# One graph layer on one core: a prelude with statistics of two rows at once, other chunks and other GpSimd shares, and an opening that runs two blocks ahead of the second unit's gather, with 22 units in place of 21

## What is computed

```python
# x (12500, 128) f32; src, dst (200000,) int32, sorted by dst
h   = relu(layernorm(x))                       # eps 1e-5
agg = segment_sum(h[src], dst, 12500) / max(deg, 1)[:, None]
h1  = relu(agg @ Wg + h @ Ws + bg)             # 128 -> 128
h2  = tanh(h1 @ W1 + b1)                       # 128 -> 512
h3  = tanh(h2 @ W2 + b2)                       # 512 -> 512
out = x + h3 @ W3 + b3                         # 512 -> 128
```

## Time and profile before

| what | value |
|---|---|
| median of 3 runs | 1659.8 us (1656.84 to 1665.99) |
| the profiled execution's own time | 1658.69 us |
| its span | 1656.8 us |
| TensorE busy | 1257.9 us, 76% of the span |
| VectorE, GpSimd, ScalarE busy | 956.5, 897.7, 552.8 us |
| mean granted TensorE clock | 0.904 of full speed |

### The profile page before, as it was taken

The page is one execution under the profiler, slowest core; times in us unless marked ns, Lnnn a source line. Parts: engine busy times, 40 slices in busy tenths (PEclk is TensorE's granted clock), DMA queues, the critical chain, the costliest instruction groups (busy, mean ns, idle before and its releaser), DMA issues.

```text
span 1656.8 us, 26502 instructions
## 1 busy us (share of the span) xinstructions
PE 1257.9 (76%) x9082; PEld 924.4 (56%) x9082; DVE 956.5 (58%) x1850; ACT 552.8 (33%) x1159; POOL 897.7 (54%) x953
## 2 busy tenths in 40 slices
PE   0204988778887888877888788888887888887888
PEld 0202656556665656565655555666555656565667
DVE  8806985546555575646556574547555665546441
ACT  6303441414142341414142341424142432324152
POOL 4473165656555655656566554656555554565530
PEclk9557999999989999888999999999988889899999
DMA  9611224142413314141414313141313313141410
GB/s 244 190 51 62 79 62 100 49 99 64 87 42 100 94 44 99 45 99 41 104 49 100 92 46 93 47 102 44 103 45 101 91 45 94 47 102 43 101 41 10
DMA packets 92829, 130.44 MB, mean 79 GB/s; under 512 B 47451, under 2 KB 73393, under 8 KB 88993
## 3 DMA queue, kind: packets, MB, share of 16 engines
q1 hardware_dynamic: 63773, 69.42, 16.3%
q0 software_dynamic: 28928, 59.30, 14.4%
HBM read 109.14 MB, written 13.09 MB: 74 GB/s over the span
## 4 chain that ended last, share of the span: by engine, by line
PE 54%; another core or an unknown queue 18%; issue 12%; ACT 8%; DVE 6%; DMA 1%; DVEq 0%; SPq 0%; ACTq 0%
PE banks L870 16%; PE banks L816 14%; PE banks L741 7%; PE banks L832 5%; PE banks L853 4%; PE banks L887 4%; DVE arena L1584 3%; ACT arena L1204 2%; ACT dense L1187 2%; ACT arena L1125 1%; PE banks L844 1%; PE banks L847 1%; ACT dense L1194 1%; PE banks L789 1%
## 5 line engine op out<-in xcount | busy, mean ns | idle before, releaser
L669 POOL DMA_INDIRECT ring<-h_table,idx_all x904 | 875.6, 969 | 670.3 <-issue 235.7
L870 PE MATMUL banks<-dense,w 128*128 128x256 f32 (+1 forms) x1568 | 430.5, 392 | 30.1 <-ACT dense L1194 16.8
L816 PE MATMUL banks<-xin,arena 128*128 128x256 f16 x2058 | 313.5, 287 | 103.9 <-issue 61.3
L1204 ACT CAST arena<-banks 128x512 f16<-128x512 f32 (+1 forms) x525 | 291.7, 579 | 206.2 <-PE banks L816 129.8
L870 PEld LDWEIGHTS banks<-dense,w 128*128 128x128 f32 x1568 | 272.2, 197 | 76.7 <-ACT dense L1194 20.8
L816 PEld LDWEIGHTS banks<-xin,arena 128*128 128x128 f16 x2058 | 190.3, 102 | 217.8 <-issue 117.4
L741 PE MATMUL banks<-ring,onehot 128*128 (+1 forms) x1008 | 194.6, 290 | 23.9 <-issue 18.1
L1574 DVE TENSOR_SCALAR arena<-arena,code_ptr 128x768 f16<-128x768 f16 (+1 forms) x336 | 133.6, 456 | 119.0 <-PE banks L816 89.6
L1584 DVE TENSOR_TENSOR arena<-node,banks 128x768 f16<-128x768 f16 (+1 forms) x168 | 152.5, 965 | 45.9 <-remote 24.7
L1194 ACT ACTIVATE dense<-banks,b2c 128x256 f32<-128x256 f32 (+1 forms) x196 | 92.0, 475 | 243.5 <-PE banks L870 125.7
L832 PE MATMUL banks<-arena 64*128 64x257 f16 x2058 | 146.5, 288 | 27.1 <-issue 21.5
(11 more groups left out here) (121 smaller groups left out, 871.2 us busy)
## 6 DMA issues: line engine op xcount, KB each, us to landing
arena<-unit_codes SPq DMA_DIRECT2D x21, 1568.0 KB
ring<-h_table,idx_all POOLq DMA_INDIRECT x904
xblk<-in_x_dram SPq DMA_DIRECT2D x48, 128.0 KB
out_dram<-dense SPq DMA_DIRECT2D x48, 128.0 KB
xin<-in_x_dram SPq DMA_DIRECT2D x4, 1232.0 KB, 17.0
h_table<-xin SPq DMA_DIRECT2D x4, 1232.0 KB
own_pair<-h_table SPq DMA_TRANSPOSE x98
w<-in_L_gnn_W_dram SPq DMA_DIRECT2D x1, 1024.0 KB
```

The source lines that it names most:

```text
L669: nc.gpsimd.indirect_dma_start(out=ring_tiles[:, t % RING, 0:2 * D], out_offset=None, in_=table, in_offset=bass.IndirectOffsetOnAxis(ap=id ...
L816: mm = nc.tensor.matmul(to, wide_l[:, piece % WSLOTS, k, j, :], tab[:, row_of(g, j), :], start=(j == 0), stop=(j == 1))
L870: mm = nc.tensor.matmul(l3_ps[c][:, 0:w], w2[:, q, c * P:(c + 1) * P], h2T[:, q, 0:w], start=(q == 0), stop=(q == HC - 1))
L1204: nc.scalar.copy(unit_msgs[:, 2 * pr:2 * pr + wide_of, 0:2 * D], unit_ps[pr % 2][:, 0:wide_of * 2 * D].rearrange("p (g d) -> p g d", d=2 * ...
```

## The change

It does the following.
- **Prelude.** Six chunks of 10, 22, 22, 18, 16 and 10 rows. `bn_stats` reads two rows at once, element by element in turn, so that its even and odd statistics are those of the two rows; the four joining instructions go. GpSimd scales 6, 12, 12, 10, 9 and 5 rows (54 of 98, before 36). GpSimd's memset of the part of x that has no rows goes, and SyncE's wait for it; other rows of x are loaded there. All of `take_idx` now follows the last chunk.
- **Opening.** Once unit 0 is gathered it is summed at once. Then its block goes through the dense layers with the steps 0 and 1 (`first_block`), and unit 1 is placed behind them. Then GpSimd's block 0 goes through the layers beside the gather of unit 1 (`first_gather`), and then unit 1's block alone beside the gather of unit 2 (`period_alone`). The second part of `split_sources`, before placed in the wait for unit 0's codes, now follows unit 0's `residual`.
- **Division.** `PB` = 27: 27 GpSimd blocks (before 28) and 22 units (before 21). `EXTRA_BEHIND` has six entries (before eight). The number of full periods (a GpSimd block and a unit's block) stays 18, from n = 3 to 20, before from n = 2 to 19; the last period is as before.

```diff
@@ -32,7 +32,10 @@
 ROWS = 22
 ROWS_OF = 98
 LAST_OF = 54
-POOL_ROWS = 8
+CHUNKS = ((0, 10), (10, 32), (32, 54), (54, 72), (72, 88), (88, 98))
+POOL_ROWS = (6, 12, 12, 10, 9, 5)
+EDGES_BEHIND = 3
+CAST_BEHIND = 3
 GT = 8
 RG = 8
 RING = RG * GT
@@ -44,8 +47,8 @@
 SUB = 128
 W = 18
 REACH = 22
-PB = 28
-EXTRA_BEHIND = (2, 4, 7, 9, 12, 14, 17, 19)
+PB = 27
+EXTRA_BEHIND = (4, 8, 12, 15, 18, 20)
 TH = 18
 UT = 2 * TH
 UCH = 2
@@ -59,10 +62,12 @@
 FIRST_UC = 100
 PAIRS_BETWEEN = (1, 1, 2, 1, 2, 2, 1, 2, 1, 1, 2, 1, 2, 1, 1, 2)
 PAIRS_ALONE = (2, 2, 2, 2, 2, 2, 2, 2, 2, 2, 2, 1, 0, 0, 0, 0)
+PAIRS_FIRST = (0, 0, 0, 0, 0, 0, 1, 1, 2, 2, 2, 2, 2, 2, 2, 2)
 AHEAD = 18
 CARRY_SLOT = 6
 TURN_SLOT = 13
 CARRY_ALONE = 3
+CARRY_FIRST = 10
 ARENA = 29320
 SCALE = 1024.0
 FAR = 32.0
@@ -128,10 +134,13 @@
 
         return m >= PB
 
-    PERIODS, EXTRA, ORDER, pool = [((), [])], {}, [], 0
+    PERIODS, EXTRA, ORDER, pool = [((0, 1), [PB])], {}, [PB], 0
     for n in range(1, UNITS):
         if n == 1:
-            PERIODS.append(((0, 1), [PB]))
+            PERIODS.append(((2,), [0]))
+            pool = 1
+        elif n == 2:
+            PERIODS.append(((3,), [PB + 1]))
         else:
             PERIODS.append(((2 * pool + 2, 2 * pool + 3), [pool, PB + n - 1]))
             pool += 1
@@ -644,17 +653,15 @@
                            allow_small_or_imprecise_dtypes=True).then_inc(iota_ready, 1)
             pool.wait_ge(iota_ready, 5)
             pool.wait_ge(ident_ready, 2)
-            nc.gpsimd.memset(xin[P - 32:P, LAST_OF:ROWS_OF], 0.0).then_inc(tail_zero, 1)
-            pool.wait_ge(tail_zero, 1)
 
             for c in range(TC):
                 s = c % 2
-                p, rows, held = chunk_rows(c)
+                _first, _rows, held = chunk_rows(c)
                 at(pool, pair_ready, c - 1)
                 pool.wait_ge(shift_ready, c + 1)
-                for r in range(min(POOL_ROWS, rows // 2 - 1)):
-                    ins = nc.gpsimd.tensor_scalar(hval[0:p, s, r, 0:D], held[0:p, r], scale[0:p, s, r:r + 1],
-                                                  shift[0:p, s, r:r + 1], ALU.mult, ALU.add)
+                for r in range(POOL_ROWS[c]):
+                    ins = nc.gpsimd.tensor_scalar(hval[:, s, r, 0:D], held[:, r], scale[:, s, r:r + 1],
+                                                  shift[:, s, r:r + 1], ALU.mult, ALU.add)
                 ins.then_inc(pool_scaled, 1)
 
             table_whole(pool)
@@ -922,14 +929,37 @@
             def end_period(n):
 
                 following = behind(n)
-                if is_unit(following):
-                    sum_unit(n, range(NP))
-                else:
-                    before_turn = WSLOTS if n == 1 else 0
-                    sum_unit(n, range(before_turn))
-                    turn(PLACE[following])
-                    sum_unit(n, range(before_turn, NP))
-                    layer1(following, PLACE[following])
+                turn(PLACE[following])
+                sum_unit(n, range(NP))
+                layer1(following, PLACE[following])
+
+            def first_block():
+
+                steps, (block,) = PERIODS[0]
+                following = PERIODS[1][1][0]
+                leads = {}
+
+                def beside_layer3(slot):
+                    if slot == 7:
+                        leads[1] = begin_sums(steps[1])
+                    if slot >= 7:
+                        sum_tiles(steps[1], leads[1], range(min(2 * (slot - 7), W), min(2 * (slot - 6), W)))
+
+                def beside_out(slot):
+                    if slot == NT * HC - 1:
+                        for c in range(UCH):
+                            place_chunk(1, c)
+
+                turn(0)
+                layer1(block, 0)
+                leads[0] = begin_sums(steps[0])
+                sum_tiles(steps[0], leads[0], range(W))
+                layer2(block, 0)
+                layer3(block, 0, beside_layer3)
+                layer4(0, 2, beside_out)
+                turn(PLACE[following])
+                turn_codes(1)
+                layer1(following, PLACE[following])
 
             def extra_block(n):
 
@@ -954,12 +984,33 @@
                 layer4(k, n + 2)
                 layer1(following, PLACE[following])
 
+            def first_gather(n):
+
+                (step,), (block,) = PERIODS[n]
+                k = PLACE[block]
+                behind_layers = sum(PAIRS_FIRST)
+
+                def beside_layer3(slot):
+                    if slot == CARRY_FIRST:
+                        carry_groups(n + 1)
+                    pr = sum(PAIRS_FIRST[:slot])
+                    gather_pairs(n, range(pr, pr + PAIRS_FIRST[slot]))
+
+                layer2(block, k)
+                layer3(block, k, beside_layer3)
+                layer4(k, n + 2)
+                gather_pairs(n, range(behind_layers, PAIRS))
+                for c in range(UCH):
+                    place_chunk(n + 1, c)
+                segment(step)
+                turn_codes(n + 1)
+                sum_unit(n, range(NP))
+
             def period_alone(n):
 
-                steps, (unit,) = PERIODS[n]
+                (step,), (unit,) = PERIODS[n]
                 k = PLACE[unit]
-                if steps:
-                    segment(steps[0])
+                segment(step)
                 turn(k)
                 layer1(unit, k)
                 layer2(unit, k)
@@ -1084,12 +1133,12 @@
             gather_pairs(0, range(PAIRS // 2 + 1))
             carry_groups(1)
             gather_pairs(0, range(PAIRS // 2 + 1, PAIRS))
-            for c in range(UCH):
-                place_chunk(1, c)
-            turn_codes(1)
-            end_period(0)
+            sum_unit(0, range(NP))
+            first_block()
             for n in range(1, UNITS):
                 if n == 1:
+                    first_gather(n)
+                elif n == 2:
                     period_alone(n)
                 elif n < UNITS - 1:
                     period(n)
@@ -1315,40 +1394,31 @@
 
             def norm_stats(c):
                 s = c % 2
-                p, rows, held = chunk_rows(c)
-                dve.wait_ge(x_in[c], 16 * len(chunk_parts(c)))
-                for r in range(rows):
-                    ins = nc.vector.bn_stats(stats[0:p, s, r], held[0:p, r])
-                ins.then_inc(stats_done, 1)
-                dve.wait_ge(stats_done, c + 1)
-                halves = [stats[0:p, s, 0:rows, k:k + 2] for k in (1, 4)]
-                nc.vector.tensor_tensor(pair_sums[0:p, s, 0:rows], halves[0], halves[1], ALU.add)
-                nc.vector.tensor_tensor(apart[0:p, s, 0:rows], halves[0][:, :, 0], halves[1][:, :, 0], ALU.subtract
-                                        ).then_inc(spread_done, 1)
-                dve.wait_ge(spread_done, 2 * c + 1)
-                nc.vector.scalar_tensor_tensor(out=variance[0:p, s, 0:rows], in0=apart[0:p, s, 0:rows], scalar=D / 4.0,
-                                               in1=apart[0:p, s, 0:rows], op0=ALU.mult, op1=ALU.mult).then_inc(spread_done, 1)
-                dve.wait_ge(spread_done, 2 * c + 2)
-                nc.vector.tensor_tensor(variance[0:p, s, 0:rows], variance[0:p, s, 0:rows], pair_sums[0:p, s, 0:rows, 1], ALU.add
-                                        ).then_inc(moments_done, 1)
+                _first, rows, held = chunk_rows(c)
+                dve.wait_ge(x_in[c], 16 * len(x_parts(c)))
+                for r in range(0, rows, 2):
+                    ins = nc.vector.bn_stats(stats[:, s, r:r + 2].rearrange("p r k -> p (r k)"),
+                                             held[:, r:r + 2].rearrange("p r d -> p d r"))
+                ins.then_inc(moments_done, 1)
 
             def norm_shift(c):
                 s = c % 2
-                p, rows, held = chunk_rows(c)
+                _first, rows, _held = chunk_rows(c)
...
@@ -1652,25 +1722,46 @@
                 if s + 2 < STEPS:
                     make_onehot(s + 2)
 
-            def period_alone(n):
-
-                steps, (unit,) = PERIODS[n]
+            def first_gather(n):
+
+                (step,), (block,) = PERIODS[n]
+                k = PLACE[block]
                 match_codes(n, [4])
                 count_earlier(n + 1)
                 match_codes(n, [5])
                 load_edges(n + 1)
                 match_codes(n, [6, 7])
-                finish(steps[0])
                 rank_edges(n + 1)
                 spread_ranks(n + 1, range(UCH))
-                make_onehot(steps[1])
                 match_nodes(n, range(WSLOTS))
-                residual(PLACE[unit])
-                add_own(PLACE[unit] + 1)
-                finish(steps[1])
+                add_own(k + 1)
+                residual(k)
+                finish(step)
                 match_nodes(n, range(WSLOTS, NP))
-                make_onehot(steps[0] + 2)
-                make_onehot(steps[1] + 2)
+                take_nodes(n + 1)
+                finish_unit(n)
```

(71 more changed lines are left out.)

180 lines of the change are left out of this document (103 added, 77 removed).

## The result

The changed kernel takes 1673.4 us (median of 5 runs, 1671.0 to 1681.8) against 1659.8 (5 runs, 1656.3 to 1666.0): ratio 1.0117, 95% interval 1.0074 to 1.016, so 12 to 27 us slower. Forecast: 1675. The profiled execution is the slowest of the five (1681.8; span 1680.0 against 1656.8), so what follows adds up to +23.2 us, not to the medians' +13.6.

The account below looks back on a forecast made before the run. No engine is full; TensorE and its hand-overs bound the middle. Prelude 0, opening +62.2 and extras -43.6 give +18.6, or +15.8 with gathers priced apart; +16.3 taken on 1658.7 gives 1675 us, range 1652 to 1692.

Parts of the forecast that it names:

- the simple way: Whole kernel: prelude 0, opening +62.2, two extra blocks fewer at 21.8 us each -43.6; sum +18.6 us.
- the second way: Whole kernel: gathers priced apart at 0.4 to 0.5 us, an extra block without its surplus gathers at 16.8; sum +15.8 us.
- The middle: Full periods: 18 stay as they are, two extra blocks go; -43.6 us, or -33.6 - 25 with gathers priced apart.
- The opening: From unit 0's gather to the first full period's layer 2: 73.1 to 135.3 us, +62.2, for two more blocks.
- The prelude: Statistics and norms before the gathers: last `norm_low` moves by -2.2 to +3.0 us; 0 taken.
- the walk through the six chunks: Prelude: chunks followed through VectorE, ScalarE and DMA; last `norm_low`, before at 59.0, ends at 56.8 or 62.0 us.
- the cheap price: Prelude: each of 49 two-row statistics takes 0.33 us, 16.3 us in all, 3.1 less than before.
- the dear end: Prelude: statistics at 0.59 us each, the interleaved read paying for line changes; +3.0 us, given one chance in two.
- The gap: Between unit 0's `place_chunk` matmuls and ScalarE's `take_q`: 53.5 us without progress of layers or units, length kept.
- the rival that it might shrink: Gap ahead of `take_q`: shrinks with the shifted start, deciding from 25 us; whole, 1622 us; nearly all of faster's 0.13.
- the opening pays for itself: Opening: overlaps like a full period and costs 50 to 53 us, total 1663 to 1666; no change, chance 0.20.
- the opening is worse: Opening: gathers and idle slow TensorE to clock 0.92, 82% busy; 135 us become 152, total 1692; chance 0.10.

Follow-up runs that it names:

- div22: The kernel before with the new division alone (27 GpSimd blocks, 22 units, six extras), old prelude and opening: 1665.5 us, ratio 1.0036.
- after_split: The changed kernel with the second `split_sources` moved back into VectorE's long wait for unit 0's codes, ahead of `take_nodes(0)`: 1672.0 us, ratio 1.0072 to the kernel before.
- after_hold13_o24: The changed kernel with GpSimd stopped behind 13 gathers until unit 0's codes, and OPEN_LOTS 24 (later gathers each await TensorE's leave): 1643.9 us, 0.9917 of the kernel before.
- hold13_24: The kernel before with GpSimd's gathers stopped behind 13 until unit 0's codes and behind 24 until unit 1's: 1652.8 us, ratio 0.9979.
- before_late: The kernel before with GpSimd issuing no gather until unit 0's codes are there: 1661.9 us, ratio 1.0036.
- after_rows: The changed kernel with fewer prelude rows for GpSimd, POOL_ROWS (3, 8, 8, 6, 5, 3): run once for its trace, 1681.1 us.

## Why the prediction was right, step by step

**The sign and the size** came from one comparison that held: two extra blocks leave the middle cheaply, and two blocks in the opening are dear. Forecast +16.3; measured +13.6 by the medians, 12 to 27 by the ratio. But both big terms of the simple way were too small, the opening by 17.9 us and the middle by 17.1. That these errors cancelled was luck in that way; the second way had both larger, for one reason, the gathers.

**The middle** was -43.6 by the simple way and -58.6 with gathers priced by themselves; it came to -60.7. The price of an extra (88 us a window) held; the windows without one fell from 66.3 to 64.7 us, with 36.6 gathers in place of 40. That is 0.5 us a gather, the price of the second way, and div22 shows that it comes with the division. The first way, which I listed first, sized it wrong: an extra's surplus gathers were paid by its neighbours, one of the signs of being wrong that the prediction names. Its 55 to 57 gathers a window with an extra don't fit all seven: counted by their starts they are 50 to 56, with a mean of 52.7, and 36 to 43 in the ten without, with a mean of 40.

**The opening** was +62.2, or +74 by the second way, and came to +80.1. Unit 0's layer 2 came 33.5 us behind the gather's start (forecast 31.6). `place_chunk(1)` took 4.4 us in place of 1.0, single matmuls 0.7 us apart beside gathers; block 0's layer 2 ran at half clock, 3.78 us; the idle ahead of unit 1's first pair was 4.5 us (forecast 7, and after_split shows its named cause right). Unit 1's layer 2 came at +105.4 (forecast 97.6). The largest miss is the period behind it: 47.8 us where I took 37.7, because I carried over unit 0's period as it was. That had 9 gathers beside it, this one has 24; 15 more at the second way's 0.4 to 0.5 us make 6 to 8 of the 10 us, an estimate. I had that price and didn't use it there. The granted clock in that period was 0.93 against 1.00; no run parts it from the gathers.

**The prelude** was 0, with bounds of -2.2 and +3.0; it is +3.9 at the last `norm_low`, outside the bounds on the dear side, although its price was the cheap one (0.34 us). The step that failed is the walk through the six chunks: it gave VectorE one wait of 4.5 us and two of 1.5 for x, and the five that came (5.9 us the longest) sum to 13.3 us, where there were 1.6 before. It also had no wait for TensorE's L717, which cost 2.3 us right ahead of the end. VectorE's work shrank as the cheap price says, and the waits ate more than that. The Trainium skill, SBUF — State Buffer, section on door 1, says that an access to another 16-byte line pays a penalty, by which the dear end would have been right. That doesn't show in this read: 256 elements alternating between two rows took 0.34 us, where 0.59 was the dear price. My second row for it, the sum at L1519, was a poor neighbour.

**The gap** was kept at 53.5 us and was 54.2. That the change "touches none of the instructions in that stretch" was reason enough for its length, but the rival that it might shrink was sized from nothing. The runs give its cause as far as the kernel can reach it, GpSimd's gathers in a row; how these hold TensorE's results up stays open.

**The rivals.** That the opening pays for itself asked that its two blocks cost 50 to 53 us; even with the gathers held back they cost 74 or more. That the whole gap goes (1622) would have needed a change in how gathers are issued, and nothing in the change makes one. after_hold13_o24 does: its first `turn_codes` comes 50.7 us earlier (87.9 in place of 138.6), and the time falls by some 30 us to 1643.9, so even then 1622 was too low. The rival "the opening is worse" was right in its term: it asked for a clock of 0.92, 82% busy and 152 us, and the opening had 0.90, 83% and 153.2. Its time (1692) missed because it kept the middle at -43.6. I gave it one chance in ten.

## What to carry to other kernels

Price a moved block by what overlaps it at its new place, not by its own length, and price the transfers issued beside it by themselves. When an engine's result is taken long after its matmuls stand as done, look at what another engine issues without a pause in that time, and hold that back by a wait; here that was worth more than the change cost. Let the engine that is slowed hand out the leave, one by one; a stop alone moves most of the loss.

## What the runs showed of the hardware

- Beside indirect gathers issued back to back (one each 1.25 us), TensorE's matmuls come one every 0.7, 1.4 or 2.8 us, the longer the run of gathers the slower (hold13_24), and one result reached ScalarE 27 us late (before_late). It begins some 6 (hold13_24) to 13 gathers (before_late) into a run and ends some 8 us or less behind it. VectorE isn't slowed: in before_late L1553 takes 1.35 us at 76.8 us, with no gather yet, and 1.35 at 139.7, beside them. The Trainium skill, SBUF — State Buffer, section SBUF: two separate sides, says of the engines' ports that TensorE never waits there on another engine; the runs don't show whether a port is where TensorE waits, only that it is slowed.
- GpSimd stands still while VectorE's `norm_low`, which reads two tensors, runs. GpSimd's rows in the changed kernel, two of them, and the 54 together:

```profile
28.55 3.80 POOL L663 TENSOR_SCALAR arena<-xin,arena 128x128 f32<-128x128 f32 x2
```

```profile
L663 POOL TENSOR_SCALAR arena<-xin,arena x54: 441/447/3376, 9.0 to 52.5; 128x128 f32<-128x128 f32 x54
```

A row takes 0.45 us, the one beside the `norm_low` of 28.96 to 32.02 took 3.38, and the one beside that of 46.06 to 48.77 took 2.74. This is the rule of the Trainium skill, SBUF — State Buffer, section SBUF: two separate sides: such an instruction of VectorE and one of GpSimd exclude each other for their whole length. On the path it cost at least 0.7 us here, by after_rows, which keeps two such rows (3.35 and 2.91 us) but lets ScalarE wait for none.
